# Attention scores as fp32 products in four row strips in place of bf16 products of split operands

## The reference, cut to what matters

```python
# layer 0, and layer 1 likewise; q and k are rotated by position first
scores = jnp.einsum('bkgtd,bksd->bkgts', Qh, Kh) / jnp.sqrt(jnp.float32(dh))   # dh = 32
scores = jnp.where(causal[None, None, None], scores, -jnp.inf)
attn = jax.nn.softmax(scores, axis=-1)
out = jnp.einsum('bkgts,bksd->bkgtd', attn, Vh)
...
# layer 1 keeps the 128 largest scores of each row and masks the others
draft = draft + jnp.where(causal_future, neg, jnp.asarray(0.0, dtype))
_, draft_indices = jax.lax.top_k(draft, num_remain)            # num_remain = 128
mask = mask.at[b_idx, h_idx, s_idx, draft_indices].set(0.0)
```

## Time and profile before

| what | us |
|---|---|
| median of 3 runs | 5173.41 |
| lowest and highest | 5171.35, 5176.51 |
| the profiled execution | 5178.51 |
| its span, first to last instruction | 5176.7 |
| first attention (478 to 1273) | 795 |
| second attention (2226 to 4785) | 2559 |

### The profile page before, as it was taken

The page is one execution under the profiler, slowest core; times in us unless marked ns, Lnnn a source line. Parts: engine busy times, 40 slices in busy tenths (PEclk is TensorE's granted clock), DMA queues, the critical chain, the costliest instruction groups (busy, mean ns, idle before and its releaser), DMA issues. The chain is left out here.

```text
span 5176.7 us, 79684 instructions
## 1 busy us (share of the span) xinstructions
PE 3755.9 (73%) x23338; PEld 2210.1 (43%) x23480; DVE 3509.0 (68%) x10383; ACT 3166.3 (61%) x7058; POOL 288.7 (6%) x213
## 2 busy tenths in 40 slices
PE   6998999998999999934555355555555555554699
PEld 2444766666444444412333233333333333332454
DVE  3654777776333356548888888888888888887444
ACT  1123777776000011259999599999999999999200
POOL 2332000000000023300000000000000000000000
PEclk9999999999999999966766566767766667766899
DMA  3325223232211112310111011110011110110222
GB/s 139 74 64 162 71 61 79 53 78 82 68 49 49 44 46 69 85 41 1 26 27 26 1 26 26 25 25 12 18 26 26 23 26 4 26 26 6 78 86 77
DMA packets 276875, 249.81 MB, mean 48 GB/s; under 512 B 170048, under 2 KB 209232, under 8 KB 276432
## 3 DMA queue, kind: packets, MB, share of 16 engines
q1 hardware_dynamic: 275888, 245.13, 18.0%
q0 software_dynamic: 544, 0.07, 0.0%
HBM read 167.56 MB, written 77.59 MB: 47 GB/s over the span
## 5 line engine op out<-in xcount | busy, mean ns | idle before, releaser
L1030 ACT ACTIVATE a_sign<-a_x,a_state 128x384 fp8e4<-128x384 f32 (+5 forms) x1536 | 1343.0, 876 | 126.3 <-DVE a_state L1166 87.9
L936 PE MATMUL a_ps_s<-k,q 128*128 128x512 bf16 (+3 forms) x1474 | 500.7, 486 | 692.0 <-DVE a_x L1267 661.7
L947 PE MATMUL a_ps_t<-ident,arena 128*128 128x128 f32 x2304 | 484.6, 355 | 194.3 <-ACT a_invT L999 130.6
L936 PEld LDWEIGHTS a_ps_s<-k,q 128*128 128x128 bf16 x1536 | 168.6, 131 | 916.3 <-DVE a_x L1267 749.8
L965 PE MATMUL a_ps_o<-a_probT,vals 128*32 128x128 f32 x4608 | 404.9, 325 | 185.1 <-ACT a_probT L995 184.7
L947 PEld LDWEIGHTS a_ps_t<-ident,arena 128*128 128x128 f32 x2304 | 338.6, 180 | 333.4 <-ACT a_invT L999 143.4
L721 ACT ACTIVATE a_prob<-a_x_neg,a_shift 128x640 f32<-128x640 f32 (+7 forms) x512 | 397.1, 776 | 80.4 <-DVE a_x_neg L764 61.9
L1267 DVE TENSOR_SCALAR_CACHE_REDUCE a_x<-a_ps_s 128x128 f32<-128x128 f32 (+7 forms) x512 | 383.7, 754 | 85.2 <-PE a_ps_s L939 59.9
L995 ACT COPY a_probT<-a_ps_t 128x512 f32<-128x512 f32 (+3 forms) x768 | 345.9, 475 | 111.1 <-PE a_ps_t L947 110.5
L764 DVE TENSOR_SCALAR_CACHE_REDUCE a_x_neg<-a_ps_s 128x640 f32<-128x640 f32 (+7 forms) x512 | 378.7, 751 | 38.8 <-PE a_ps_s L645 25.6
L1177 DVE MAX8 a_nine<-a_below 128x8 f32<-128x256 f32 (+6 forms) x448 | 371.0, 828 | 32.9
(11 more groups left out here) (216 smaller groups left out, 5947.7 us busy)
## 6 DMA issues: line engine op xcount, KB each, us to landing
q<-qk SPq DMA_DIRECT2D x256, 256.0 KB, 4.9
qk<-p_qkT SPq DMA_DIRECT2D x32, 960.0 KB, 6.2
h_rows<-h SPq DMA_DIRECT2D x32, 512.0 KB, 6.8
k<-qk SPq DMA_DIRECT2D x256, 64.0 KB, 5.2
m_o<-o SPq DMA_DIRECT2D x32, 512.0 KB, 5.5
m_h<-h SPq DMA_DIRECT2D x32, 512.0 KB, 5.3
h<-tok_h SPq DMA_DIRECT2D x16, 512.0 KB, 4.0
arena<-in_wo SPq DMA_DIRECT2D x16, 512.0 KB, 11.3
```

The source lines that it names most:

```text
L936: nc.tensor.matmul(ps_s[:, n % 2, a:a + w], q[:, y, head, i * P:(i + 1) * P], k[:, y, a:a + w], start=(y == 0), stop=False, skip_group_che ...
L947: mm = nc.tensor.transpose(ps_t[:, (n + 1) % 3, c:c + P], prob[:, par, at:at + P], ident[:, :])
L1030: ins = nc.scalar.activation(to, x[:, par, at:at + w], ACT.Sign, scale=-1.0, saturate=False, bias=state[:, par, 0, n:n + 1], accum_out=sta ...
```

## The change

Queries and keys stay fp32 and are not split. The projection transposes 10 blocks of fp32 a tile, straight from `rot`, and GpSimd's program there is gone. `load_queries_keys` puts the queries of two heads in strips 0, 1 and strips 2, 3, and the same keys in all four. `pair_scores` makes one query tile of two heads at once: strip r does head r // 2 and half r % 2 of the key columns, with 32 rows, into a bank of its own; the bias follows with all 128 rows. So a pair fills all four banks of `ps_s`, and a fetch reads two banks. In the first attention TensorE makes steps s + 2 and s + 3 ahead of `turn(s)`, for even s; in the second, the fetches go by pairs (tile by tile, both heads), and keeps and gathers are sorted anew around them.

```diff
-SPLITS = 3
-Q_PARTS = ((0, 0, 0, 1), (1, 2, 1, 2))
-K_PARTS = ((0, 1, 2, 0), (1, 0, 2, 1))
+STRIPS = P // DH
...
-        TURNS = chunks(SPLITS * QK, 2 * BANK)
+        TURNS = chunks(QK)
...
                 def qk_transposes(j, par):
-                    pe.wait_ge(parts_ready, j + 1)
                     if not (isinstance(j, int) and j == 0):
                         pe.wait_ge(qkT_ready, j * NQ)
                     for t, (a, n) in enumerate(TURNS):
-                        if t >= 3:
-                            pe.wait_ge(qkT_ready, j * NQ + (t - 2))
+                        pe.wait_ge(rope_done, j * 3 + (t + 1))
                         for c in range(0, n, P):
-                            m = nc.tensor.transpose(ps_qk[:, t % 3, c:c + P], part[:, par, a + c:a + c + P],
-                                                    ident_b[:, :])
+                            m = nc.tensor.transpose(ps_qk[:, t, c:c + P], rot[:, par, a + c:a + c + P], ident[:, :])
...
-            @block.gpsimd
-            def _(pool):
...
                     if n == 0 and not (isinstance(j, int) and j < 2):
-                        dve.wait_ge(parts_ready, j - 1)
+                        dve.wait_ge(qkT_done, (j - 1) * NQ)
...
+    heads = qk_dram[ds(q_at, P), ds(t_at, T)].rearrange("(y m d) t -> m d y t", m=2, d=DH)
+    for r in range(STRIPS):
+        rows = slice(r * DH, (r + 1) * DH)
+        sp.dma_start(q[rows, :, :], heads[r // 2]).then_inc(arrived, 16)
+        sp.dma_start(k[rows, :], qk_dram[ds(k_at, DH), ds(t_at, T)]).then_inc(arrived, 16)
+
+
+def pair_scores(nc, ps, q, k, i, ident_b, bias_b):
+    half = (i + 1) * P // 2
+    for r in range(STRIPS):
+        rows, m, a = slice(r * DH, (r + 1) * DH), r // 2, r % 2
+        nc.tensor.matmul(ps[:, m, a, 0:half], q[rows, i * P:(i + 1) * P], k[rows, a * half:(a + 1) * half], start=True,
+                         stop=False, tile_position=(r * DH, 0), skip_group_check=True)
+    done = []
+    for m in range(2):
+        for a in range(2) if i == 0 else (1,):
+            c, w = (0, half) if i == 0 else (half - P, P)
+            at = a * half if i == 0 else 0
+            last = nc.tensor.matmul(ps[:, m, a, c:c + w], ident_b[:, :], bias_b[:, at:at + w], start=False, stop=True,
+                                    skip_group_check=True)
+        done.append(last)
+    return done
...
-                        wait_met(pe, shift_ready, at(STEPS, s - 1))
...
+                        wait_met(pe, shift_ready, at(STEPS, s))
+                        for done in pair_scores(nc, ps_s, q[:, x, m // 2, :], k[:, x, :], i, ident_b, bias_b):
+                            done.then_inc(s_done, 1)
...
                     for s in range(STEPS):
+                        if s % 2 == 0 and (s + 2 < STEPS or not last):
+                            scores(s + 2)
                         turn(s)
-                        if s + 3 < STEPS or not last:
-                            scores(s + 3)
...
+    PAIRED = [(m, i) for i in range(TT) for m in range(2)]
+    RANKED_PAIRED = [RANKED.index(t) for t in PAIRED if t[1]]
...
+                        if not (isinstance(s, int) and s < 0 and i == 0):
+                            pe.wait_ge(x_ready, (s + 1) * (2 * TT) + 2 * i)
+                        for done in pair_scores(nc, ps_s, q[:, 1 - par, :], k, i, ident_b, bias_b):
+                            done.then_inc(s_done, 1)
...
-                    KEEPS = [(), (), range(0, TT - 1), range(TT - 1, NS - 2), range(NS - 2, NS)]
-                    FETCHES = [(), (), range(0, 4), range(4, 12), range(12, 2 * TT)]
-                    GATHERS = [(), (), (), range(0, 3), range(3, NS - 4)]
+                    KEEPS = [(), (), RANKED_PAIRED[:8], RANKED_PAIRED[8:12], RANKED_PAIRED[12:]]
+                    FETCHES = [(), (), range(0, 6), range(6, 12), range(12, 2 * TT)]
+                    GATHERS = [(), (), (), RANKED_PAIRED[:8], RANKED_PAIRED[8:]]
...
                         elif p > 2:
-                            for k in range(max(len(keeps), len(fetches))):
-                                if k == len(keeps):
+                            for r in keeps[:2]:
+                                keep(r).then_inc(prob_ready, 1)
+                            keeps, gathers = keeps[2:], gathers if p == 3 else gathers[:2]
+                            dve.drain()
+                            for k in range(0, max(len(keeps), len(fetches)), 2):
+                                for n in fetches[k:k + 2]:
+                                    fetch(n)
+                                for r in keeps[k:k + 2]:
+                                    keep(r).then_inc(prob_ready, 1)
+                                if k >= len(keeps):
                                     dve.drain()
...
+                                for n in share(gathers, k // 2, len(fetches) // 2) if fetches else ():
                                     gather(n, y)
+                                if k < len(keeps):
+                                    dve.drain()
```

111 lines of the change are left out of this document (28 added, 83 removed).

## The result

The changed kernel takes 5421.35 us (median; 5418.07 to 5423.27) against 5174.96 (5171.35 to 5176.78) for the kernel before, measured beside it. The ratio is 1.0476, 95% interval 1.0458 to 1.0495: slower by 246 us. The forecast was slower, 5346 us, range 5225 to 5440.

What follows compares the result with a forecast made beforehand. TensorE was taken to bound the first attention and projections, ScalarE and VectorE the second attention. 5178.5 + 95 (first attention) + 130 (second) - 52 (projections) = 5351.5, on the median's scale 5346 us; range 5225 to 5440.

Steps and rivals of the forecast that it cites:

- the lost second score buffer: Both attentions: TensorE may not start a pair before VectorE fetched both heads; wait 0.55 + 0.107(i+1) us at 2.4 GHz.
- the level race of ScalarE and VectorE: Second attention, passes 2 and 3: ScalarE's counts wait for VectorE's thresholds, so longer VectorE parts lengthen the slot, 4.2 us.
- TensorE's rate alone: Rival: TensorE's rate sets the first attention, -50 us there, second +30, projections -52: 5101 us; chance 0.12.
- strips in turn: Rival: strips don't run together, column terms four times as large, first attention +370 more, second +380 more: 6095; chance 0.03.
- The first attention, +95 forecast: First attention: four units grow from 48.5 to 54.4 us, 5.9 more, times 16; bounds -30 and +150.
- the four unit lengths: First attention, units of a long and a short tile, four heads each: 13.95, 13.8, 13.05, 13.65, together 54.4 us.
- short to short: First attention, unit (7,0): time from the first short pair's first fetch to the second's, 2.75 us.
- long to short: First attention, unit (7,0): from the second long pair's first fetch to the first short pair's, 5.55 us.
- The second attention, +130 forecast: Second attention: passes 2 to 4 make each slot 4.2 us longer, 31 slots; bounds +85 and +160.
- the one slot in which rows are chosen exactly stays as it is: Second attention: the single slot with the exact row choice was to add nothing to the forecast.
- Projections, -52 forecast: Projections: ten fp32 transposes for 30 bf16 give -32 us over 32 tiles, the ends -20; bounds -35 and -60.
- first attention even: Rival: in the first attention the saved columns go into switches and waits, no more; 5241 us, chance 0.12.

Runs made afterwards that it cites:

- order_alone: Kernel before with only the change's instruction order and single score buffer, products still bf16 in three parts, projections unchanged: 5420.63 us.
- strips_twice: Changed kernel with each pair's four strip products issued twice, the second overwriting the first with the same values: 5661.76 us.
- heads_apart: Changed kernel's data and strips, but one head (two strips) at a time in the old TensorE order, second buffer back: 5421.61 us.
- switch_between: strips_twice with a one-column product over all 128 rows between the two rounds, adding a tiling switch out and back per pair: 5812.94 us.
- split_by_two: Kernel before with fp32 projection transposes, bf16 split afterwards on GpSimd, each projection's last tile split by VectorE: 5177.31 us, ratio 1.0008.

## Why the prediction was right, and where it was off

**Direction.** It rested on the lost second score buffer being dearer than the saved columns, and on the level race of ScalarE and VectorE in the second attention. Both hold: idle time before the fetches appears where it was put, released by the bias product, and ScalarE idles before its counts in passes 3 and 4. Neither "TensorE's rate alone" nor "strips in turn" is seen in any kernel.

**The price of strips and switches.** Right in each term at 2.4 GHz: 0.107(i+1) us a pair, 0.10 in, 0.10 for weights (0.09 forecast), 0.12 out (0.15 forecast). The prediction had the earlier trace rows at 1.2 GHz; the trace's record of the granted clock begins only at 82.5 us, after the token map, so this is read from durations, 0.853 us for 512 fp32 columns there and 0.43 in the projection (48 in 20.84 us). In a unit of (7,0) the first long pair's fetch and the first short pair's were forecast 9.35 us apart (3.8 and 5.55); the median is 9.38.

**The first attention, +95 forecast, +124 measured.** The step that was too small is the sum of the four unit lengths, 54.4 us: it is 57.2 on average, of single units 14.5, 15.0, 13.1 and 13.3 as medians for 13.95, 13.8, 13.05 and 13.65. Undisturbed it is 55.0 (14.51, 14.07, 13.11 and 13.32), and 16 times 0.6 are some 10 of the 29 us. In (7,0) the term that was too small is short to short, 3.34 us for 2.75; long to short is 5.60 for 5.55. The other 19 us are a thing that the sum had not: it was worked out at 2.4 GHz throughout. Five units of (7,0), each at a loop's jump back, took 16.7 to 18.3 us. One of them by windows (columns of the earlier trace rows) and in TensorE's timeline:

```profile
1020.60:1022.60 2.00, 0.56 (x6) 0.32 (x3) 2.00 (x5) 1.66 (x3) 0.00 (x0) 1.00 0.07 16
1022.60:1024.60 2.00, 0.36 (x4) 0.37 (x8) 0.64 (x3) 0.22 (x3) 0.00 (x0) 0.73 0.00 0
1024.60:1026.60 2.00, 2.00 (x11) 0.50 (x8) 0.00 (x0) 1.19 (x2) 0.00 (x0) 0.50 0.05 16
1026.60:1028.60 2.00, 2.00 (x11) 1.70 (x10) 1.34 (x3) 0.79 (x2) 0.00 (x0) 0.50 0.00 0
```

```profile
1024.24 2.09 PE L482 MATMUL a_ps_s<-k,q 32*128 32x512 f32 x8 [3.08 <-issue]
1026.26 0.39 PE L489 MATMUL a_ps_s<-a_bias_b,a_ident_b 128*128 128x128 bf16 x2
1026.45 3.91 PE L640 MATMUL a_ps_t<-ident,a_prob 128*128 128x128 f32 x16
```

TensorE stands 3.08 us after the jump, the granted clock falls to 0.50, and the strips and sixteen transposes of a tile 7 pair take twice their time. TensorE also pauses 2.2 to 2.5 us at the jumps in order_alone, where the clock of the stage stays 0.99; in the changed kernel a pause of 1.44 to 1.92 us in three units of four comes on top (48 of over 1.2 us in the stage, for 6 in order_alone), and it is 0.95. The lengths that the units have beyond their undisturbed ones sum to 33.5 us against 14.3 in order_alone: 19 us, all of the 18.6 that the strips cost there. That the pauses bring the low clock is argued. For it: apart from the stretches in which the stage begins and ends there are 21 at 0.50, and each begins in one of these pauses or at most 1.6 us after it. But the pauses alone do not settle it: strips_twice has as many (49), with TensorE idle as long in all (165 us for 168), but 11 such stretches; heads_apart has only 5 pauses and still 33.1 us beyond its undisturbed units, all of it in units of (7,0). By windows, strips_twice and then heads_apart:

```profile
450.00:1480.00 1030.00, 856.59 (x11712) 578.15 (x11704) 591.40 (x1536) 601.05 (x1472) 25.65 (x64) 0.98 0.17 45
```

```profile
446.00:1354.00 908.00, 887.15 (x9665) 567.33 (x9662) 603.32 (x1536) 608.93 (x1472) 25.80 (x64) 0.97 0.19 51
```

Why a pause is followed by 0.50 in one unit and not in another stays open.

**What was credited wrongly.** The prediction put the whole loss on the buffer. The order costs a third of it in either attention even with both buffers (42.7 of 124.2, 59.8 of 177.3), in the sequence in which the kernels were built. Its sums had the order in them (they were laid out instruction by instruction), so the size came out; the reason was told too simply.

**The second attention, +130 forecast, +177 measured.** 128 us are the 31 slots, 4.1 us each for 4.2, and 7 lie outside them: the first slot's thresholds are ready 30.0 us after the stage's first product for 21.9, since there the pairs are scored with no other work over their waits, which the sum had left out. Pass by pass it is close: VectorE's parts of passes 2, 3 and 4 grew from 9.4 to 9.9, 10.8 to 12.6 and 8.6 to 9.6 us in the slots shown, for +1.4, +1.7 and +1.1 forecast; ScalarE's periods, the measure of what it costs, grew by 1.0, 1.8 and 1.0 (medians). Pass 2 was costed too high, about half of it by a gap of 0.74 after the branch that is now 0.27. The remaining 42 us break the sentence "the one slot in which rows are chosen exactly stays as it is". The branch depends on values, and the strips add the products in another order and precision, so one tile more, of 640 columns, does not come to its count of rows by thresholds. That is argued; what is shown is the count: all six kernels with strips have 32 MAX8 there, all kernels with bf16 products have 16. With it the second attention went over the bound of +160, which was made for waits alone.

**Projections, -52 forecast, -57 measured.** -1.04 us a tile for -0.99, the ends 3 us better in all.

**The sum.** The misses, +29, +47 and -5, come to +71 in the stages, of the 75 us between 5346 and 5421, which is inside the range. The range held by the width that the unknown prices of waits had asked for, not by any place kept for a second long slot or for a low clock in the first attention: that 61 us of such terms fitted into it is luck. (One rival's time was added up wrongly: "first attention even" gives 5251 by its own terms, 5173.4 + 130 - 52, not 5241; nothing hangs on it.)

**Open.** Whether strips would pay with a second buffer for the short tiles alone was not tried, and no run here shows whether two pairs can lie in the four banks at once.

## What to carry to other kernels

Half the columns were worth nothing here, where the product stands between the last fetch of one pair and the first of the next: count what the new form does to the buffers and the order first, then the columns. To see what a bundle of edits costs, build the order alone with the old arithmetic: here it had 245 of the attentions' 302 us. And where the code branches on values, a change in how sums are rounded can be a change in the work; the count of the rare branch's instructions is the row to look at.

## What the runs showed of the hardware

In switch_between a change of TensorE's tiling cost 0.10 to 0.12 us each way and a reload of weights 0.10 at 2.4 GHz, 0.32 in all with a one-column product between. Four fp32 row strips ran at the full factor of four at both clock levels (a round of 256 columns 0.213 us at 2.4 GHz, of 512 columns 0.853 at 1.2). Inside the changed kernel's first attention the granted clock fell to 0.50 21 times, each time in a pause of TensorE of 1.44 to 3.08 us or at most 1.6 us after it, and there were 48 such pauses; a stage with as many pauses had it 11 times (strips_twice). VectorE's subtraction of two SBUF inputs took 2.93 us for 0.69 beside GpSimd's. And at a loop's jump back VectorE stood still for 2.8 to 3.1 us in all but the two kernels with split_by_two's edit, where it was 5.0 to 5.3, worth 28 us in a stage that no edit touched; so a difference of 0.5% between two kernels can come from somewhere else than the edit, and only the trace by stage tells.
